# Building the normalised, transposed input inside the attention block of a two-sequence transformer layer

## What is computed

```python
def _layernorm(x, axis=-1, eps=1e-5):
    m = jnp.mean(x, axis=axis, keepdims=True)
    v = jnp.var(x, axis=axis, keepdims=True)
    return (x - m) / jnp.sqrt(v + eps)

q = (resid_pre @ Wq.T).reshape(b, s, H, DH)      # H = 16 heads of DH = 128; k and v alike
scores = jnp.clip(einsum('bqhd,bkhd->bhqk', q, k) / sqrt(DH), -1024, 1024)
attn = softmax(scores + alibi_and_causal_mask)
z = einsum('bhqk,bkhd->bqhd', attn, v)
out = einsum('bqhd,ohd->bqo', z, Wo.reshape(d, H, DH))
```

## Time and profile before

| | us |
|---|---|
| the two runs shown | 4609.22 and 5025.45, median 4817.34 |
| the profiled execution | 4612.62 |
| span of its slowest core (core 2) | 4610.8 |
| spans of the other cores | 4578.6 to 4604.3 |
| stage A1 of sequence 0, core 2 | from 6.2 (first load) to 117.5 |
| stage A1 of sequence 1, core 2 | from 2313.7 to 2423.9 |

### The profile page before, as it was taken

How to read it: one execution, slowest core, us unless ns; L and a number is a source line. 1 busy time by engine, 2 the same in 40 slices (tenths; PEclk the granted TensorE clock), 3 DMA queues, 4 the chain that set the end, 5 groups by cost and what they waited for, 6 DMA issues and landing times. The chain is left out here.

```text
span 4610.8 us, 71951 instructions; the slowest of 8 cores (4578.6 to 4610.8 us)
## 1 busy us (share of the span) xinstructions
PE 3848.1 (83%) x18452; PEld 1820.2 (39%) x18452; DVE 1664.4 (36%) x4528; ACT 1140.6 (25%) x2608; POOL 543.4 (12%) x1106
## 2 busy tenths in 40 slices
PE   2889899989988696788828898999899986967888
PEld 1334344444444242344413343444344443423444
DVE  2343453454445111233323434544544451112333
ACT  6242332232223100011162323422332231000111
POOL 4010110011000101011140101100110001010110
PEclk9878778877887797788858788778778877977888
DMA  5111101110110646321151111011101106562111
GB/s 163 24 19 19 24 15 19 20 19 15 19 24 1 143 155 137 79 82 74 65 169 24 19 19 24 15 17 21 19 15 19 20 5 142 158 141 80 74 74 74
DMA packets 55562, 258.79 MB, mean 56 GB/s; under 512 B 13720, under 2 KB 13984, under 8 KB 34720
## 3 DMA queue, kind: packets, MB, share of 16 engines
q0 software_dynamic: 36464, 119.66, 12.9%
q1 hardware_dynamic: 14128, 100.98, 6.7%
q10 hardware_dynamic: 4608, 33.56, 2.1%
HBM read 273.15 MB, written 67.11 MB: 74 GB/s over the span
## 5 line engine op out<-in xcount | busy, mean ns | idle before, releaser
L819 ACT ACTIVATE prT<-dg,cstt 128x128 bf16<-128x128 f32 (+1 forms) x576 | 216.2, 386 | 1851.8 <-POOL dg L791 1546.7
L780 DVE TENSOR_SCALAR sp<-ps 128x512 f32<-128x512 f32 (+3 forms) x1104 | 627.8, 594 | 101.2 <-ACT prT L844 24.6
L771 PE MATMUL ps<-QT,KT 128*128 128x512 bf16 (+3 forms) x1104 | 492.6, 478 | 143.1 <-DVE sp L780 60.5
L714 PE MATMUL pz<-va,prT 128*128 128x129 bf16 x3652 | 552.4, 264 | 55.3 <-ACT prT L819 29.1
L1070 PE MATMUL cb<-wf,cT 128*128 128x512 bf16 x2048 | 519.2, 418 | 83.8 <-DMA wf<-wf 69.0
L844 ACT ACTIVATE prT<-sp,cstt 128x128 bf16<-128x128 f32 (+2 forms) x1368 | 577.2, 487 | 0.2
L420 PE MATMUL bp<-wo,zTt 128*128 128x512 bf16 x2048 | 462.3, 390 | 79.5 <-DMA wo<-wo 79.5
L627 PE MATMUL pp<-xnT,wv 128*128 128x512 bf16 x2048 | 493.3, 406 | 2.4 <-PEq L298 2.0
L714 PEld LDWEIGHTS pz<-va,prT 128*128 128x128 bf16 x3652 | 374.6, 103 | 278.6 <-issue 194.0
L627 PE MATMUL pp<-xnT,wq 128*128 128x512 bf16 x2048 | 447.3, 379 | 0.0
L627 PE MATMUL pp<-xnT,wk 128*128 128x512 bf16 x2048 | 447.3, 379 | 0.0
(11 more groups left out here) (106 smaller groups left out, 2390.9 us busy)
## 6 DMA issues: line engine op xcount, KB each, us to landing
a1x<-x SPq DMA_DIRECT2D x32, 1024.0 KB, 6.1
bx<-x SPq DMA_DIRECT2D x32, 1024.0 KB, 6.4
x2d<-b POOLq DMA_DIRECT2D x32, 1024.0 KB, 8.4
c<-x2d ACTq DMA_DIRECT2D x32, 1024.0 KB, 4.8
out<-co SPq DMA_DIRECT2D x32, 1024.0 KB, 3.9
wq<-wq POOLq DMA_DIRECT2D x32, 512.0 KB, 6.0
wk<-wk POOLq DMA_DIRECT2D x32, 512.0 KB, 5.6
wv<-wv POOLq DMA_DIRECT2D x32, 512.0 KB, 6.1
```

The lines of the kernel that those rows point to most:

```text
L714: lambda e, ps_=ps_, c=c, c0=c0, qt=qt: e.matmul(pz[qt % 2][:, 0:129], probsT[:, ps_: ps_ + 128], vaug[:, c * VSLOT: c * VSLOT + 129], sta ...
L771: lambda e, c=c, q0=q0, n=n, bank=bank: e.matmul(psc[bank][:, 0:n], KT[:, c * 128:(c + 1) * 128], QT[:, q0 * 128: q0 * 128 + n], start=Tru ...
L780: lambda e, n=n, bank=bank, buf=buf: e.tensor_scalar(spanb[buf][:, 0:n], psc[bank][:, 0:n], 1024.0, -1024.0, ALU.min, ALU.max),
L819: soff=soff: e.activation(probsT[:, pslot:pslot + min(ncols, 128)], diagb[:, soff:soff + min(ncols, 128)] if ncols == 64 else diagb[:, 0:128],
```

## The change

The block of stage A1 goes, and its work is put at the head of stage A2's block, before the first head is planned. Three things differ from the work that was there before:

- Buffers: `xbuf` and `xnb` have two buffers each instead of four. They are now slices of `probsT`, which stage A2 has anyway and which no head uses until its first exponential. The load of tile i waits for the apply of tile i-2, and the Square of tile i for the transposes of tile i-2.
- PSUM: all transposes go through `ptp`, one bank, so each group of four waits for the copy of the group just before it.
- Waits: every projection matmul of head 0 waits for the copies that it reads, of the last tile of its token group (192 waits for each sequence). There is no end of a block between the last copy and the first projection.

The weights of head 0 are sent in the order V, Q, K rather than Q, K, V, after the memset of `vaug`. The loops' order is that of before: all 16 tiles, then head 0.

```diff
-        with ExitStack() as a1es:
-            xbuf = [a1es.enter_context(nc.sbuf_tensor(f"a1x{s}{i}", [P, D], F32))
-                    for i in range(4)]
-            xnb = [a1es.enter_context(nc.sbuf_tensor(f"a1n{s}{i}", [P, D], BF16))
-                   for i in range(4)]
-            cc = a1es.enter_context(nc.sbuf_tensor(f"a1c{s}", [P, 32], F32))
-            pt = [a1es.enter_context(nc.psum_tensor(f"a1p{s}{i}", [P, 512], BF16))
-                  for i in range(2)]
...
-            with nc.Block() as blk:
-                pg.run_block(blk)
...
+            pf32 = bufs["probsT"].bitcast(F32)
+            xbuf = [pf32[:, 0:2048], pf32[:, 2048:4096]]
+            cc = pf32[:, 4096:4112]
+            xnb = [bufs["probsT"][:, 12288:14336],
+                   bufs["probsT"][:, 14336:16384]]
+            for w_d, w_sb in ((dram["wv"], wv_sb), (dram["wq"], wq_sb),
+                              (dram["wk"], wk_sb)):
...
+            apply_tok = [0, 0]
+            xnb_guard = [0, 0]
+            cp_tok = [[0] * 4 for _ in range(NT)]
+            for i in range(NT):
+                bb = i % 2
+                ld = pg.op("sync",
+                           lambda e, i=i, bb=bb: e.dma_start(
+                               xbuf[bb], x_d.ap()[s][i]),
+                           inc=sem["dxa"][bb], amt=16,
+                           waits=[(s_pool, apply_tok[bb])])
+                t8 = _plan_ln(pg, xbuf[bb], xnb[bb], xnb[bb], cc, 8 * bb,
+                              sem, (sem["dxa"][bb], ld),
+                              [(s_pe, xnb_guard[bb])], eng="gpsimd")
+                apply_tok[bb] = t8
+                last_t = 0
+                for g in range(4):
+                    for j in range(4):
+                        dc = g * 4 + j
+                        w = []
+                        if j == 0:
+                            w = [(s_pool, t8), (s_dve, st["ptp_copy"])]
+                        last_t = pg.op(
+                            "tensor",
+                            lambda e, bb=bb, dc=dc, j=j: e.transpose(
+                                bufs["ptp"][:, j * 128:(j + 1) * 128],
+                                xnb[bb][:, dc * 128:(dc + 1) * 128],
+                                sb["idb"][:, :]),
+                            inc=s_pe, waits=w)
+                    ct = pg.op("vector",
+                               lambda e, i=i, g=g: e.tensor_copy(
+                                   bass.AP(xnT, (4 * g) * SEQL + i * 128,
+                                           [[NDC * SEQL, P], [SEQL, 4],
+                                            [1, 128]]),
+                                   bufs["ptp"][:, 0:512]),
+                               inc=s_dve, waits=[(s_pe, last_t)])
+                    st["ptp_copy"] = ct
+                    cp_tok[i][g] = ct
+                xnb_guard[bb] = last_t
+            st["xnT_cp"] = cp_tok
...
@@ -618,6 +600,8 @@
             for dc in range(NDC):
                 w = []
+                if h == 0:
+                    w.append((s_dve, st["xnT_cp"][4 * tg + 3][dc // 4]))
                 if dc == 0:
```

More of the change, by code:

```diff
@@ L353, in _build_seq @@
                       ptp_copy=0, ztr_tok_pe=[0, 0], pend_z=[])
+            pf32 = bufs["probsT"].bitcast(F32)
[5 more added lines that the diff above has]
+                              (dram["wk"], wk_sb)):
+                wi = {id(wq_sb): 0, id(wk_sb): 1, id(wv_sb): 2}[id(w_sb)]
+                wtok[0][wi] = pg.op(
+                    "gpsimd",
+                    lambda e, w_d=w_d, w_sb=w_sb: e.dma_start(
+                        w_sb[:, :],
+                        w_d.ap()[0].rearrange("p c o -> p (c o)")),
+                    inc=sem["wpre"][wi], amt=16)
```

## The result

The changed kernel takes 4651.05 us (median of its runs; its profiled execution 4648.48) against 4614.27 before: a ratio of 1.0081, 95% interval 1.0069 to 1.0092. It is slower by 0.8%, about 37 us.

What follows compares the result with a forecast made beforehand. PE, busy 3848.1 of 4610.8 us, was taken as the bound, stage A1 as bound by the ACT-POOL exchange. Terms 15.7 + 17.0 + 3.8 + 2.0 - 2.6 = +35.9 us on 4612.62 gave 4648, range 4610 to 4692.

Steps and rivals of the forecast that it cites:

- from the sum to the chances: Chances: loss of 15 to 60 us 0.84; with 2% as threshold, same 0.90, slower 0.08, faster 0.02.
- Overlap, none: Stage A1 into head 0: all 256 transposes precede the first projection, so none of PE's 80.5 us idle is filled.
- Two input buffers: Stage A1: with loads of 5.5 us, tile pairs take 14.52 us against 12.34; +15.7 and +17.0 us for the sequences.
- The start term: Start of each sequence: tile 2's load shares with the weight loads and lands later; +1.9 us a sequence, +3.8 in all.
- One PSUM bank and no block end: End of stage A1: last tile's transposes to first projection take 4.3 us instead of 3.28; +1.0 us a sequence.
- 192 waits, 0: Head 0's projections: waits already fulfilled cost nothing; 0 taken, at most 2 us a sequence.
- Table load: Before head 0's first exponential: one ACT_TABLE_LOAD goes, since A1 ends with an Exp; -1.28 us a sequence.
- Clock, 0: Head 0's V projection: slow first matmuls as before, 16.4 us for 64; 0 taken, bounds -2.3 to +12 a sequence.
- things that it named as proof: Trace signs: Squares 7 to 7.5 us apart, PE's apply wait about 15 us longer, stretch after A1 unchanged, among others.
- Rival A: Stage A1: head 0's projections fill PE's gaps; about 4585 us, or 4540 if loads hide too; chance 0.03.
- B: Stage A1: loads return early enough, so it keeps 6.17 us a tile; 4610 us; chance 0.05.
- C: Stage A1: loads come back late throughout, at 13.6 us each; slower by over 2%, 4757 us; chance 0.06.

## Why the prediction was right and wrong

The mechanism held for the stage, and the time came out as given: 4648 forecast, 4651 measured; +35.9 us forecast, 37 measured. That the total agrees so well is partly luck, as the terms show. Wrong was what the prediction made of this number.

**Where it failed.** The step that failed is the one from the sum to the chances. The prediction put its own loss at 15 to 60 us and then counted it as no change, with 0.90 on that and 0.08 on slower, by the sentence that differences within 2%, 92 us, are about what a measurement here can't tell. The runs show otherwise: the interval of the ratio, 1.0069 to 1.0092, is 0.23% wide, and the 37 us stand clear of it. The prediction had what it needed to see this: 4609.22 and 4612.62 were 3.4 us apart, and its own 0.3% between executions is 14 us, less than half of the loss that it forecast. So +36 us should have been called a slow-down.

**The luck in the total.** All terms of the sum lie between a sequence's first Square and head 0's first exponential. There the forecast had +35.9 us and the runs show +30.1, so it was 5.8 too high. Another 5 to 8 us came from outside that stretch, from heads and later stages that the prediction took as unchanged, and nearly filled the gap.

**Term by term.**
- Overlap, none: right. PE's idle time grew, and no V matmul stands ahead of the last transposes. The run with the order changed in PE's list shows that the list was the obstacle: 62 us came in the two stages for 64 worked out.
- Two input buffers, +32.7 and +3.8 for the starts: measured +31.5 in all from first to last Square (14.5 and 17.0). The chain was right, the load was mis-sized: 5.5 us was taken between 4.9 and 6.0. Over tiles 7 to 15 the median load took 4.8 to 5.0 us on every core in sequence 0 and 4.9 to 5.4 in sequence 1, with longer ones, up to 6.9, on some tiles. Core 2, with 6.0 in the earlier trace rows, had 5.0; the row of the other cores was the better one. The start term was +1.9 a sequence; the first pair is longer than the later ones by 1.6 us in sequence 0 and 0.2 in sequence 1.
- The page of the Trainium skill that was weighed, DMA: Bandwidth & Descriptors (Anatomy of one DMA), gives 4.4 us for 1 MB, an estimate by its formula, which that section fits to transfers sent by GpSimd; the loads here are sent by SyncE. It would have made the two terms 17.3 us instead of 32.7. The measured 4.9 lies between that and the value taken, and the measured sum is nearer to the value taken.
- One PSUM bank and no block end, +1.0 a sequence: measured +0.9 (13.3 against 12.4). The bound it set on the Squares, 13.4 us a pair, showed as 13.6 once a third input buffer had taken the loads off the path.
- 192 waits, 0: confirmed within 0.1 us over the 64 V matmuls.
- Table load, -1.28 a sequence: PE's wait fell by 1.30. The Trainium skill's ScalarE activation tables (Table sets in the compiler and the runtime) says per block, and the trace agrees: one load fewer in each sequence.
- Clock, 0: right in head 0, not beyond it. The V projection of head 0 takes 15.5 us before and after (16.4 had been worked out), but seven later heads of sequence 0 take some 4 us longer, where head 8 starts at the lower clock on core 1, and this was nowhere in the sum.

Of the things that it named as proof, two did not come. PE's wait for the apply was to be about 15 us longer and is 15 to 20 us shorter, core by core in sequence 0. The waits for the single bank, 32.5 us against 4.0, lengthen a tile's transposes and leave less of the gap before the next apply; the two waits together are 8 to 14 us longer. "The stretch after A1 unchanged" did not come true, by the 5 to 8 us above. The others held: Squares 7.1 and 7.2 us apart on average, ACT idle for the loads, groups 1.26 us apart, no table load ahead of head 0's exponential.

Rival A needed an order that the kernel did not have; B failed on the loads; C did not come: from tile 3 on no load took over 7 us, in either sequence.

## What to carry to other kernels

Moving a stage's operations in front of the next stage's in the same in-order lists overlaps nothing: waits allow an order, the list makes it, and only when the matmuls were put between the transposes did PE's idle time fill. Where a stage's buffers are cut, add up how long one is held (from first read to last read, the hand-over, the load) and compare it with the number of buffers times the pace: here 13.9 us for two input buffers against 12.2; a third covers that, and then the two normalised tiles hold the pair at 13.6. Compare the forecast with the spread that the executions show, here 3.4 us between the two at hand, not with a general bound: 0.8% was plain to see.

## What the runs showed of the hardware that was not expected

With the same instructions in the same order, the instant at which the granted clock rises at the start of a head differs between kernels that differ only in a stage that ended over 600 us earlier: on core 1 1.00 against 0.80 over the first 9 us of head 8, and in the mean of the cores 4 us over seven heads. It differs between the cores of one kernel too: 639.2 to 644.5 us for these heads in the kernel before. Moved weight loads cost more than they had at the start: 5.8 us over six pairs of sequence 0 for three transfers (2.6 in sequence 1), when only two input buffers are there. And a block end with its table load cost 3 us a sequence where the trace's own rows, 1.00 and 1.28, had suggested 2.3.
